# Identity products on TensorE ahead of the first transposes of a fused cross-attention and mixture-of-experts kernel

## The reference

```python
x = x + xattn(ctx, layernorm(x), mask, mask, W_src, b_src, W_tgt, b_tgt, W_out, b_out)
x = x + ffn(layernorm(x), gate_w, w_gate, w_up, w_down, sw_gate, sw_up, sw_down)

# xattn: k, v = split(ctx @ W_src.T + b_src) ; q = layernorm(x) @ W_tgt.T + b_tgt
#        8 heads of 32, masked softmax(q k / sqrt(32)) v, then
#        concat(layernorm(x), update) @ W_out.T + b_out
# ffn:   weights of the 8 best of 16 sigmoid scores, normalised, times
#        (silu(x @ w_gate) * (x @ w_up)) @ w_down, plus the shared expert
```

## Time and profile before

| | |
|---|---|
| Time, median of 3 runs (lowest to highest) | 1078.71 us (1078.62 to 1082.48) |
| The profiled execution | 1080.32 us, of which 1078.1 us span from the first to the last instruction |
| PE busy in the span | 1020.2 us (95%), 5198 matmuls |
| DVE, ACT, POOL busy | 643.9, 474.9, 389.5 us |
| Mean granted TensorE clock | 0.981 of full speed |

### The profile page before, as it was taken

How to read it: one execution, slowest core, us unless ns; L and a number is a source line. 1 busy time by engine, 2 the same in 40 slices (tenths; PEclk the granted TensorE clock), 3 DMA queues, 4 the chain that set the end, 5 groups by cost and what they waited for, 6 DMA issues and landing times.

```text
span 1078.1 us, 14971 instructions
## 1 busy us (share of the span) xinstructions
PE 1020.2 (95%) x5198; PEld 778.1 (72%) x5198; DVE 643.9 (60%) x1497; ACT 474.9 (44%) x871; POOL 389.5 (36%) x355
## 2 busy tenths in 40 slices
PE   2889999999999997889999999999999999999998
PEld 2656667676667664547888888888888888888886
DVE  6777777777777663434555555565555555555544
ACT  3257575656565654655433323233333333333232
POOL 2378797879797974426410010010010010100000
PEclk9989999999999996989999999999999999999999
DMA  6443433424242223213323032121121220220320
GB/s 214 108 134 77 136 76 113 126 63 133 70 114 70 66 55 88 95 51 115 89 70 88 21 99 67 50 79 59 52 85 42 70 79 30 82 77 23 102 70 22
DMA packets 65610, 87.87 MB, mean 82 GB/s; under 512 B 10656, under 2 KB 31024, under 8 KB 65536
## 3 DMA queue, kind: packets, MB, share of 16 engines
q1 hardware_dynamic: 63936, 85.09, 27.3%
q10 hardware_dynamic: 1600, 1.84, 0.5%
HBM read 56.97 MB, written 4.46 MB: 57 GB/s over the span
## 4 chain that ended last, share of the span: by engine, by line
PE 54%; POOL 0%; ACT 0%; issue 0%; DVEq 0%; DVE 0%
PE ps L644 34%; PE pst L644 17%; PE ps L650 1%; PE ps L802 1%; PE ps L803 0%; PE ps L800 0%; POOL ut_l L1374 0%; DVEq L1399 0%; DVE x L1166 0%; ACT ut_h L859 0%; ACT yt L859 0%; DVE ob L1296 0%
## 5 line engine op out<-in xcount | busy, mean ns | idle before, releaser
L644 PE MATMUL ps<-x_h,weights 128*128 128x512 f32 x1088 | 366.4, 398 | 0.8 <-DVE x L1166 0.8
L644 PEld LDWEIGHTS ps<-x_h,weights 128*128 128x128 f32 x1088 | 205.2, 189 | 50.3 <-DVE x L1166 1.0
L1173 DVE TENSOR_REDUCE mx<-ps 128x1 f32<-128x512 f32 x256 | 173.4, 685 | 91.4 <-PE ps L723 90.5
L859 ACT ACTIVATE hh<-qb 128x512 fp32r<-128x512 f32 x136 | 86.0, 632 | 293.6 <-DVE qb L1277 281.4
L644 PE MATMUL ps<-x_l,weights 128*128 128x512 f32 x544 | 215.1, 395 | 0.0
L1272 DVE TENSOR_TENSOR qb<-ps,sg 128x512 f32<-128x512 f32 x136 | 94.1, 692 | 189.8 <-PE ps L644 179.4
L644 PE MATMUL pst<-hh,weights 128*128 128x512 f32 x544 | 194.7, 399 | 1.4 <-ACT e_buf L859 1.4
L859 ACT ACTIVATE e_buf<-pst 128x512 f32<-128x512 f32 x256 | 147.2, 596 | 98.2 <-PE pst L739 87.4
L1279 DVE TENSOR_TENSOR hl<-qb,hh 128x512 fp32r<-128x512 f32 x136 | 94.3, 693 | 95.0 <-ACT hh L859 95.0
L1369 POOL TENSOR_TENSOR e_sums<-e_sums,e_buf 128x1024 f32<-128x1024 f32 x60 | 143.5, 2391 | 12.5 <-ACT e_buf L859 6.6
L739 PE MATMUL pst<-q_stack,k_stack 98*128 98x512 f32 x256 | 109.8, 432 | 20.6 <-ACT e_buf L859 20.6
(11 more groups left out here) (153 smaller groups left out, 1399.6 us busy)
## 6 DMA issues: line engine op xcount, KB each, us to landing
cb<-combine_scratch SPq DMA_DIRECT2D x128, 256.0 KB, 3.2
q_stack<-q_h SPq DMA_DIRECT2D x128, 64.0 KB, 2.0
k_stack<-k_h SPq DMA_DIRECT2D x124, 64.0 KB, 2.0
ctx_raw<-in_ctxT SPq DMA_DIRECT2D x7, 1024.0 KB, 5.6
x<-in_x SPq DMA_DIRECT2D x8, 512.0 KB, 4.2
q_stack<-q_l SPq DMA_DIRECT2D x64, 64.0 KB, 2.0
out_x<-ob SPq DMA_DIRECT2D x16, 256.0 KB, 2.2
k_stack<-k_l SPq DMA_DIRECT2D x62, 64.0 KB, 2.0
```

The costliest lines, as they stand in the source:

```text
L644: ins = engine.matmul(dst, lhsT, rhs, start=start and n == 0, stop=stop and n == len(terms) - 1)
L859: return engine.activation(dst, src, func, **kw)
L1173: engine.tensor_reduce(MX[:, g % 2, h // 2, h % 2, q:q + 1], bank(step), AX.X, ALU.max).then_inc(sem("max"), 1)
```

## The change

Behind PE's wait for the identity and ahead of its first step stand 28 matmuls of the identity with itself, fp32, 128x128 by 128x128, each starting and stopping its own accumulation in the first 128 columns of the bank `OP`. Nothing reads them, nothing waits for them, and no semaphore is counted up. All else is as before.

```diff
 FIRST_UNITS = 6
 LAG = 2
+
+WARM = 28
 NH = LAG + 1
@@ tensor_program
             pe.wait_ge(sem("ld_ident"), 16)
+            for _ in range(WARM):
+                engine.matmul(OP[:, 0:128], ID[:, :], ID[:, :], start=True, stop=True)
             for step in ORDER:
                 kind = step[0]
                 if kind == "turn_x":
```

## The result

The changed kernel is slower: 1083.76 us (median of 14 runs, 1082.23 to 1085.22) against 1080.68 for the kernel before on the same chips, a ratio of 1.0029 (95% interval 1.0019 to 1.0039), about 3 us. The kernel before has a wide spread of its own, 1078.1 to 1084.4 in the batches of the experiments (23 to 33 runs each; one run of 5627 us here and one of 3842 us in the batch of e4 are left out); two of the three runs shown ahead of the prediction lay at its lower end. The fastest of these 14 runs of the changed kernel is 4 us above the fastest of before, the slowest 1 us above the slowest; in e10, 12 further runs of it, the fastest is 1080.96.

What follows compares the result with a forecast made beforehand. PE bounds the kernel, busy 95% of the span, with phase two a fixed block from 492.91 us. Products cost 0 and faster transposes gain 0.3 us: 1078.71 - 0.3 = 1078.4 us, range 1075.9 to 1082.5.

Steps and rivals of the forecast that it cites:

- Products, their price and place: PE's start: 28 products, each 0.43 us at the lower clock, 0.22 at the upper, from 5.9 to 13.5 to 15.0 us.
- The clock: PE before `q`: clock rises during the products, is lost before `q`; faster transposes gain 0 to 0.6 us, middle 0.3.
- list of falls: Four stretches ahead of clock falls, PE busy 0.10 of 3.3 to 1.57 of 2.9 us, cited for losing it before `q`.
- The products themselves cost nothing ... They have no DMA: PE's start: the products end before the transposes at 16.49 us, covered by idle time, without DMA or semaphore: 0 us.
- Carried on: the next steps follow each other without slack: From `q` through `f_buf` to `v` at 26.81 us: each step waits for the last, so 0.3 us counts in full.
- The level: Whole kernel: 1078.71 us, median of three runs before, as the base from which the gain was subtracted.
- my forecast of the difference: Whole kernel: 0.3 us faster, from transposes at the upper clock; chance 0.60.
- the clock holds up to `q`: Rival, transposes through `q` and first `k`: upper clock kept, 2.0 us sooner, 1076.7 us; chance 0.20.
- The late rival: PE's start: products overrun 16.49 us and delay the transposes; 1080.1 us, or 1081.9 at the high price; chance 0.08.
- my rivals: Whole kernel: clock holds, 1076.7 us (0.20); nothing moves, 1078.7 (0.12); products late, 1080.1 to 1081.9 (0.08).
- the rise of the clock coming later in one run than in another: After `q` has begun: the rise may vary by up to a us or two between executions; nothing put on it.

Runs made afterwards that it cites:

- e4: Kernel before plus 222 already-met semaphore waits (111 instructions) on PE ahead of the wait for the identity, no products; ratio 1.0027 to the kernel before.
- e10: The changed kernel with its 28 products run again, nothing altered; ratio 1.0026 to the kernel before.
- e2: Changed kernel with 7 products of 512 columns instead of 28 of 128, same PE work; median 1080.43 us, ratio 0.9992 to the kernel before.
- e6: Kernel before plus 9 products of 512 columns at the start and, behind the transposes, one of 512 and one of 256; ratio 0.9971 to the kernel before.
- e12: e6 run again, in the batch of e11; ratio 0.9973 to the kernel before.
- e5: Changed kernel with all 28 products plus 176 met waits (88 instructions) ahead of the wait for the identity; median 1083.46 us, ratio 1.0009 to the kernel before.
- e1: Kernel before with 112 no-operations on PE in place of the products; they were not in the program that ran; ratio 1.0008 to the kernel before.
- e3: Kernel before with 256 no-operations on PE in place of the products; they were not in the program that ran; ratio 0.9999 to the kernel before.
- e8: e6 with its first 9 products of 512 columns cut into 36 of 128; ratio 1.0010 to the kernel before.
- e9: e4 with half the met waits (108, 54 instructions), no products; ratio 1.0014 to the kernel before.
- e11: Changed kernel plus 3 products of 512 columns ahead of the tenth scores matmul, in PE's idle stretch; ratio 1.0001 to the kernel before.
- e7: e2 plus 3 products of 512 columns ahead of the tenth scores matmul; median 1080.38 us, ratio 0.9983 to the kernel before.

## Why the prediction was wrong

- **Products, their price and place: right.** There are 56 records of 0.21 and 0.11 us, two to a product. They start at 6.05 us (forecast 5.9) and end at 13.97 (forecast 13.5 to 15.0).
- **The clock: right.** It rose during the products, was lost ahead of `q` after 1.09 us of work in 5.4 us, and came back at 22.7 us. The transposes ran at the upper level and `f_buf` was 0.5 us early (forecast 0 to 0.6). The prediction's list of falls left out two of the six ahead of the last us, those at 53.6 and 459.8 us, and with the first of them the cold stretch of 53.6 to 60.5 us, whose place matters for the next bullets.
- **"The products themselves cost nothing ... They have no DMA": the step that failed.** It put the products at 0 us from the engine's idle time and the DMAs that the kernel issues, and left out the program: some 111 instructions more shift every later fetch of PE's program. Measured, they cost 3 us (1.0029, and 1.0026 in e10). Nothing of it stands in the products' own 8 us. e4 shows the loss without any product (1.0027), e2 and e6 show products without the loss.
- **"Carried on: the next steps follow each other without slack": it held, but was looked at too briefly.** I followed the chain to 27 us and assumed the rest. The 0.5 us were still there at 56 us, on PE and on SP (0.52 us), and e12 carries 1.9 us to the end. But from 50 to 66 us SP's row of issues sets the pace: a delay of 1.1 us in it took away more than had been won, and PE's lead of 2.8 us at 63 us was worth nothing and only made the idle stretch longer in which the clock was lost.
- **The level.** 1078.71 was the median of three runs, two of them at the low end of a kernel that spreads over 6 us; later batches gave medians of 1080.68 to 1082.35. The range took 1082.48 as the end of that spread. From the right level my forecast of the difference, -0.3 us, would have read 1080.4, and still have missed by over 3 us.
- **Rivals.** That the clock holds up to `q` was worth 2.0 us by my sum; brought about in e6, it brings `f_buf` 1.75 us forward and the whole 3 us. The late rival, in e5, moved `f_buf` by 1.5 us and the time by about 1 us by the ratio, whose interval includes no change. None of my rivals had the mechanism that decided. The prediction also put nothing on the rise of the clock coming later in one run than in another; it came at 22.9 us in the profile of before and at 25.3 to 25.4 in e1 and e3, the same work.

What is shown and what isn't. That more instructions on PE, and not the products or their clock, bring the loss is shown by e4 and by the two pairs e2 with the changed kernel and e6 with e8. That the way is a fetch beside an SP issue is shown less directly: in each of the changed kernel, e4, e8, e9, e10 and e11 a fetch on q8 falls beside an SP issue in a row of stack issues, and that issue takes 1.25 to 2.0 us instead of 0.59; in e1, e2, e3, e5, e6, e7 and e12 no fetch falls on the row of 48 to 66 us, and none of its issues is long (e12 has one long issue in the earlier row, at no cost). Taken over phase one in all 14 traces, 162 of 186 stack issues that began while a fetch was under way took 0.95 us or more, and one of some 4900 with no fetch near. Why the issue waits is not seen, and the two runs that moved the fetches out of the row of 48 to 66 us by met waits (e5, e9) don't decide. That the delay of about 1.1 us grows to about 3 through the clock rests on e11 (1.0029 and 1.0026 to 1.0001), on the profiles of e4 and e10, in which PE idles 2.8 and 2.2 us instead of 1.5 and then runs at the lower level, and on the spread: the executions of 1078 to 1080 us that the kernel before has are missing in the changed kernel. The clock is also lost there with no delayed issue, as in e1, e2, e3 and e6, and e5 kept it through 3.3 us of idle time; that the delay makes the loss the rule is argued from the spread, not counted.

## What to carry to other kernels

Filler work is not free merely because its engine is idle: it lengthens that engine's program, and the fetch of the program can fall on another engine's DMA issues. So make filler of few, wide instructions (7 of 512 columns instead of 28 of 128) and look where the instruction queue's packets fall. Keep the filler going up to the moment of use, through every gap ahead of it: filler that ended 5.4 us ahead of `q` gave 0.5 us here, filler that held the clock up to it 1.75. Where a kernel has modes of its own by where its cold stretches fall, take the level from many runs, and follow a gain to the next resource that sets the pace.

## What the runs showed of the hardware

- A fetch of 16 KB of PE's program beside a DMA issue of SP goes, in nearly all cases, with an issue of 0.95 to 2.2 us instead of 0.59. The kernel before has a dozen such places too (1.39 us at 175.5 us and 1.26 at 194.4 us, for instance). Most cost nothing: from 75 to 400 us the changed kernel has them at other places than before, and its distance to before stays within 0.1 us of 2.7. The Trainium skill, page "Runtime: NRT & Kernel Launch", section "Instruction fetch mechanics", has the blocks of 16 KiB and calls their cost mostly hidden; for SP's issues beside them the traces show otherwise.
- The record of the granted clock says 1.00 until the first rise, while distances of 0.43 us for 512 columns show the lower level (21.7 to 22.6 us of the profile of before, rise at 22.9).
- Met waits on PE are not free: with 176 of them ahead (88 instructions by my count) the first product started at 10.79 us instead of 6.05 (e5).
